# Mixture-of-experts rows gathered over two batches: 15 expert tiles per pair of batches in place of 22, with the gather and the final product one loop iteration later

## The chip, the cores and the metric

One core of a Trainium2 chip runs one program. The metric is the device time in microseconds of that core, as the median of several executions. The program is written instruction by instruction for five engines, which run in parallel and wait for each other on semaphores: TensorE (PE: matmuls and transposes), VectorE (DVE), ScalarE (ACT), GpSimd (POOL) and SyncE (SP, which here only issues DMAs). An engine takes its own instructions strictly in the order in which they are written.

## The reference

Eight batches of 512 tokens with 128 features pass two layers, everything in float32.

```python
x = L0_attn_x                                   # (8, 512, 128)
xn = _layernorm(x)
s = _L0_attn_ref(xn, Wq, bq, Wk, bk, Wv, bv)    # attention, diagonal masked
g = _silu(_L0_ffn_ref(xn, gate, W1, b1, W2, b2))  # 8 experts 128->256->128, top 2 of 8 mixed by gates
x = x + s * g
xn = _layernorm(x)
s = _L1_attn_ref(xn, ...)                       # state-space layer: rmsnorm, conv, scan over the tokens
g = _silu(_L1_ffn_ref(xn, centroids, gamma, beta, W1, b1, W2, b2))
x = x + s * g
```

The scan of `_L1_attn_ref` is, for 256 channels with 16 states each, `s = s * exp(d_t * A) + d_t * B_t * u_t` over the 512 tokens of a batch, and `y = sum over states of s * C_t`. The second experts (`_L1_ffn_ref`), which the change concerns, send each token to one of 8 experts:

```python
scores = feats @ centroids.T
expert = jnp.argmax(scores, axis=1)
alpha = jax.nn.sigmoid(jnp.sum(feats * centroids[expert], axis=-1, keepdims=True))
# per expert: layernorm, gamma, beta, 128 -> 512, relu, 512 -> 128, residual
y = the row of the token's own expert
out = alpha * y + (1.0 - alpha) * feats
```

## The kernel before

**Stages.** The work of a batch is cut into steps of five groups: A (layer norm, attention and first experts), H (projections of the state-space layer, and the choice of the second expert), S (the scan), F (the second experts) and C (the end of the state-space layer, the product and the output). The main loop has one iteration per batch: while S of batch b runs, the engines also work on A of batch b+2, H of batch b+1, F of batch b and C of batch b-1. Before the first scan stands an opening in which only A and H of the first batches run, and behind the last scan an end. I call the iteration in which batch b is scanned iteration b, 0 to 7. Iteration 6 has almost no A left and iteration 7 has neither A nor H.

**What sets the order.** A table `ROWS` gives every step a place in time and an offset for ACT, DVE and POOL, with the PSUM bank it uses. `OWN` and `OWN_BANKS` replace these for batches at the start. `PLACES` sorts all steps of all batches, and `program(engine)` is the resulting order of one engine. Nothing is decided when the program runs. There are four working banks `work0` to `work3`.

**The scan.** A batch has 32 scans, two halves h of the channels for each of 16 states n. For each, PE spreads a row of B over the partitions (`b_row`, L898), DVE multiplies (`dbu` or `b_row` by `du`, L1346), ACT makes the decays (`dA`, L988, the line of a helper that all of ACT's work has), DVE scans (L1357), and POOL multiplies by C (L1539). The rows of C are fetched from DRAM by SP (L685, tile `Cs`, three buffers). PE adds the first half in `yacc` (L915, in the last iteration L912) and POOL the second (L1546, in the last iteration PE, L938). Few state buffers exist, so a scan waits until the product of an earlier state has been added.

**The second experts.** After DVE has chosen an expert per token it computes, in step `rk` (L1307 to L1321), how many tiles of 128 rows each expert needs and at which row each token goes. 512 tokens over 8 experts need at most `ST` = (512-8)//128+8 = 11 tiles. POOL scatters the rows to `xs_dram` (L1509, four indirect DMAs, steps `put`). SP loads the tiles four at a time (L696, L670) and copies the expert's first weights within SBUF for each tile (L667, `hs<-w_w1f`). PE turns the rows (L868), multiplies (L875, eight matmul records per tile), ACT applies relu (`hsT`), PE multiplies again (L883 the bias, L885 eight records), ACT copies (`ys`), SP stores to `ys_dram` (L678), and POOL gathers the rows of the tokens back (L1526, four indirect DMAs, steps `get`, tile `fe`). ACT scales by alpha, POOL adds (L1518), ACT takes tanh, DVE finishes silu (L1334, result `g1`), and after PE's output projection (L947) DVE adds and multiplies (L1385, L1388), POOL or at the very end DVE adds the kept x (L1563, L1392), and SP stores (L709).

**Preparation.** DVE scales the weights `w1f` by gamma in SBUF (L1431), adds a bias (L1436) and splits another (L1421 to L1425). `xs_dram` is zeroed by three DMAs (L721).

## Time and profile before

| what | value |
|---|---|
| device time, median of 3 runs | 944.47 us (940.72 to 945.70) |
| the profiled execution | 945.51 us |
| its span, first to last instruction | 943.7 us |
| PE busy | 815.7 us, 86% of the span |
| DVE busy | 799.8 us, 85% |
| ACT busy | 630.5 us, 67% |
| POOL busy | 597.8 us, 63% |
| mean granted PE clock | 0.934 of 2.4 GHz |
| first scan starts, last scan ends | 123.44 us, 927.15 us |

A busy share is an average over the whole span. The windows further below give it by stage. The page counts matmuls from a model of their ends, so an engine that is shown busy for a mean of 290 ns per small matmul has issued them faster than that, and a timeline row with several in a group gives their pace. The chain that ended last goes by shares of the span: PE 42%, DVE 36%, issue 12%, ACT 5%, POOL 3%.

### The profile page before, as it was taken

How to read it: one execution, taken by the hardware profiler on the slowest of the kernel's cores; microseconds unless marked ns; L12 is line 12 of the kernel's file. 1: busy time of each engine (PE TensorE's matmuls, PEld its weight loads, DVE VectorE, ACT ScalarE, POOL GpSimd, SP SyncE). 2: the span in 40 equal slices, each digit the busy share in tenths (PEclk: the TensorE clock that was granted, in tenths of full speed). 3: DMA queues.
4: the chain of work that ended last, by engine and by line, in shares of the span. 5: the costliest groups of instructions: out<-in, count | busy, mean ns of one | idle time of the engine just before them, and what ended most of it. 6: DMA issues, size and time to landing. Idle time of an engine off the chain costs nothing.

```text
span 943.7 us, 16309 instructions
## 1 busy us (share of the span) xinstructions
PE 815.7 (86%) x4844; PEld 607.9 (64%) x4844; DVE 799.8 (85%) x1487; ACT 630.5 (67%) x1378; POOL 597.8 (63%) x564
## 2 busy tenths in 40 slices
PE   4999989986999799987899779997999876775995
PEld 3785767674686577775676657765776755563662
DVE  3345789998989979998899989899899899988995
ACT  3535678766686757776687766867677675666561
POOL 0010327578575876679584876758765797879774
PEclk9989999998999879998899979998899998977998
DMA  7300232243232431333222332324222432343441
GB/s 259 107 2 0 70 95 84 62 129 100 77 107 73 124 90 53 111 113 106 85 88 79 118 95 68 120 76 124 82 73 71 122 112 91 99 133 111 144 135 41
DMA packets 79433, 90.32 MB, mean 96 GB/s; under 512 B 8451, under 2 KB 49907, under 8 KB 78835
## 3 DMA queue, kind: packets, MB, share of 16 engines
q1 hardware_dynamic: 77298, 85.07, 29.2%
q0 software_dynamic: 2048, 4.20, 1.6%
q8 instruction: 42, 0.69, 0.3%
q14 instruction: 45, 0.36, 0.1%
HBM read 52.96 MB, written 13.04 MB: 70 GB/s over the span
## 4 chain that ended last, share of the span: by engine, by line
PE 42%; DVE 36%; issue 12%; ACT 5%; POOL 3%; DMA 1%; SPq 1%; DVEq 0%; POOLq 0%; ACTq 0%
DVE st L1357 10%; PE work L850 9%; PE work L844 9%; DVE b_row L1346 4%; PE work L777 3%; DVE cv L1270 3%; DVE acc L1241 3%; PE work L875 3%; DVE dbu L1346 2%; PE work L885 2%; PE work L761 2%; PE yacc L915 2%; PE work L768 2%; POOL st L1539 1%; PE yacc L977 1%
## 5 line engine op out<-in xcount | busy, mean ns | idle before, releaser
L1539 POOL TENSOR_TENSOR st<-st,Cs 128x512 f32<-128x512 f32 x249 | 317.2, 1280 | 161.1 <-DVE st L1357 159.3
L988 ACT ACTIVATE dA<-delta,Aneg 128x512 f32<-128x512 f32 x256 | 176.2, 722 | 14.1 <-DVE st L1357 10.4
L1357 DVE TENSOR_TENSOR_SCAN st<-dA,dbu 128x512 f32<-128x512 f32 x128 | 154.8, 1210 | 0.7 <-ACT dA L988 0.7
L844 PE MATMUL work<-xnT,w_w1a 128*128 128x512 f32 x256 | 137.2, 626 | 16.8 <-DVE delta L1327 15.0
L1357 DVE TENSOR_TENSOR_SCAN st<-dA,b_row 128x512 f32<-128x512 f32 x123 | 148.8, 1210 | 3.1 <-ACT dA L988 2.9
L850 PEld LDWEIGHTS work<-w_w2a,hid 128*128 128x128 f32 x1024 | 131.3, 205 | 18.2 <-issue 15.0
L850 PE MATMUL work<-w_w2a,hid 128*128 128x128 f32 x1024 | 134.2, 288 | 3.5 <-ACT hid L988 3.5
L1546 POOL TENSOR_TENSOR y<-y,st 128x512 f32<-128x512 f32 x105 | 133.5, 1271 | 5.2
L988 ACT ACTIVATE hid<-work,w_b1a 128x512 f32<-128x512 f32 x128 | 87.9, 688 | 66.7 <-PE work L844 60.3
L988 ACT ACTIVATE hsT<-work,hs 128x128 f32<-128x128 f32 x352 | 99.2, 372 | 45.0 <-PE work L875 45.0
L875 PEld LDWEIGHTS work<-xsT,hs 128*128 128x128 f32 x704 | 98.8, 209 | 24.3 <-DVEq L1246 9.6
L1346 DVE TENSOR_TENSOR dbu<-b_row,du 128x512 f32<-128x512 f32 x123 | 85.4, 694 | 30.8 <-PE b_row L898 22.3
L875 PE MATMUL work<-xsT,hs 128*128 128x128 f32 x704 | 104.0, 295 | 8.3 <-DVEq L1246 7.2
L885 PE MATMUL work<-w_w2f,hsT 128*128 x704 | 102.5, 290 | 0.0
L1241 DVE SCALAR_TENSOR_TENSOR acc<-work,gates,acc 128x128 f32<-128x128 f32 x256 | 71.2, 341 | 34.2 <-PE work L850 34.0
L885 PEld LDWEIGHTS work<-w_w2f,hsT 128*128 128x128 f32 x704 | 88.3, 197 | 3.2 <-issue 1.2
L1346 DVE TENSOR_TENSOR b_row<-b_row,du 128x512 f32<-128x512 f32 x123 | 83.9, 682 | 2.7
L915 PE MATMUL yacc<-w_ident,st 128*128 128x128 f32 x448 | 72.6, 291 | 3.6 <-POOL st L1539 3.6
L915 PEld LDWEIGHTS yacc<-w_ident,st 128*128 128x128 f32 x448 | 59.2, 155 | 20.4 <-issue 15.2
L1509 POOL DMA_INDIRECT xs_dram<-ht_tok,pos x32 | 32.2, 1006 | 61.8 <-DVE pos L1321 55.5
L844 PEld LDWEIGHTS work<-xnT,w_w1a 128*128 128x128 f32 x256 | 42.7, 198 | 37.1 <-DVE delta L1327 20.0
L898 PE MATMUL b_row<-bc,sel_b 96*128 96x512 bf16 x123 | 49.3, 401 | 14.3 <-DVE st L1357 14.2
(198 smaller groups left out, 1315.4 us busy)
## 6 DMA issues: line engine op xcount, KB each, us to landing
Cs<-c_dram SPq DMA_DIRECT2D x128, 256.0 KB
hs<-w_w1f SPq DMA_DIRECT2D x88, 258.0 KB, 2.3
xs_in<-xs_dram SPq DMA_DIRECT2D x16, 256.0 KB
ys_dram<-ys SPq DMA_DIRECT2D x16, 256.0 KB, 3.7
w_w1f<-in_w1f_dram SPq DMA_DIRECT2D x1, 2064.0 KB, 8.4
x_in<-in_x_dram SPq DMA_DIRECT2D x8, 256.0 KB, 3.1
w_w2f<-in_w2f_dram SPq DMA_DIRECT2D x1, 2048.0 KB, 12.2
kept_dram<-x_tok SPq DMA_DIRECT2D x8, 256.0 KB, 3.5
```

The costliest lines, as they stand in the source:

```text
L844: last = mm(w[:], W["w1a"][:, i * 128:(i + 1) * 128], xnT[:], start=True, stop=True)
L850: last = mm(w[:, t * 128:(t + 1) * 128], hid[:, c % 4, t * 128:(t + 1) * 128], W["w2a"][:, c * 128:(c + 1) * 128], start=(c == PER * i), s ...
L875: last = mm(w[:, c * 128:(c + 1) * 128], w1s[:, i % 2, c * 128:(c + 1) * 128], xsT[:, i // 4 % 2, i % 4 * 128:(i % 4 + 1) * 128], start=Tr ...
L885: last = mm(r, hsT[:, i % 2, c * 128:(c + 1) * 128], W["w2f"][:, bass.ds(e * H1 + c * 128, 128)], start=False, stop=(c == HC - 1))
L898: mm(rows_bank(n, b)[:], row_of(n), bc3[:, par], start=True, stop=True).then_inc(sig["B_in"], 1)
L915: add = mm(yacc[:, t * 128:(t + 1) * 128], state(s)[:, t * 128:(t + 1) * 128], ident[:], is_transpose=True, start=(n == 0 and t == 0), sto ...
L988: return nc.scalar.activation(out, in_, func, **k)
L1241: last = V.scalar_tensor_tensor(acc[:, t], w[:, t * 128:(t + 1) * 128], gates[:, t, i:i + 1], acc[:, t], ALU.mult, ALU.add)
L1346: V.tensor_tensor((dbu0, rows_bank(n, b))[h][:], rows_bank(n, b)[:], du[:, par, h], ALU.mult).then_inc(sig["dBu"], 1)
L1357: V.tensor_tensor_scan(state(s), dA[:, s % DECAYS], (dbu0, rows_bank(n, b))[h][:], 0.0, ALU.mult, ALU.add).then_inc(sig["scan"], 1)
L1539: G.tensor_tensor(state(s), state(s), Cs[:, b.of(NS, n) % C_BUFS], ALU.mult).then_inc(sig["P"], 1)
L1546: G.tensor_tensor(y1[:], y1[:], state(s), ALU.add).then_inc(sig["y_sum1"], 1)
```

## The change

- F now runs once per **pair** of batches. 1024 tokens need at most (1024-8)//128+8 = 15 tiles, so `ST` is 15 and there are 4 pairs in place of 8 batches: 60 tiles in place of 88.
- The rows go to a fixed place in DRAM: every expert has room for 8 tiles (`ROOM`), and the second batch of the pair continues behind the first. `xs_dram` has 71 slots, twice, and all are zeroed by 18 DMAs each, in place of 3 in all.
- After the second batch of a pair DVE computes which slot is which tile (`tile_table`: `texp`, `slot`, and the row of each token among the 15 tiles, `gpos`). `rk` of the first batch is shorter.
- SP loads each tile by a DMA of its own, with its slot read from SBUF.
- The prepared weights `w1f` are saved in DRAM (`w1f_dram`, one store of 2.1 MB) and fetched from there for each tile. Their place in SBUF then holds `g1`, two more buffers of `xn1`, two of the output `ox`, and `xr`.
- Gather, silu, product and output are a new group G, which for batch b runs in iteration b+2 (before: gather at the end of iteration b, product in b+1). G of batches 6 and 7 therefore stands at the end of the program.
- `op` only adds (into `ox`, L1483); the product is a step `fin`.
- All numbers of `ROWS`, `OWN` and `OWN_BANKS` are new. F of pair 3 and G of batches 5, 6 and 7 have tables of their own.

How many tiles' first products (L875, now L938) PE has in each iteration, counted in its order: before 11 in each of the eight; after 0, 9, 6, 9, 6, 9, 6, 15 in iterations 0 to 7.

```diff
-ST = (T - E) // 128 + E
+PAIRS = NB // 2
+ROOM = 2 * T // 128
+ST = (2 * T - E) // 128 + E
+SLOTS = E * ROOM + ST - 2 * T // 128
...
-    ("P", "dve", 0, -4.05984, 0, -9, 3, None),
+    ("P", "dve", 0, -4.69974, 0, -5, 3, None),
...
+    ("P", "save", 0, 0.01296, 1, 0, 0, None),
...
-AHEAD = {"A": 2, "H": 1, "S": 0, "F": 0, "C": -1, "P": 0}
+AHEAD = {"A": 2, "H": 1, "S": 0, "C": -1, "G": -2, "P": 0}
+COUNT = {"F": PAIRS, "P": 1}
...
+        g1, xn1_c, xn1_d, ox_a, ox_b, xr = (W["w1f"][:, k * T:(k + 1) * T].rearrange("p (i d) -> p i d", i=NT) for k in range(6))
+        ox = ox_a, ox_b
...
-                        sp.dma_start(w1s[:, k % 2], W["w1f"][:, bass.ds(e * (H1 + HC), H1 + HC)]).then_inc(w_ld[k % 2], 16)
+                        sp.dma_start(w1s[:, k % 2], w1f_dram[bass.ds(e * D, D)]).then_inc(w_ld[k % 2], 16)
...
+                        for i in group_tiles(k):
+                            r = sp.value_load(slot[0:1, par, i:i + 1], min_val=0, max_val=SLOTS - 1)
+                            sp.dma_start(xs_in[:, i % 4], xs_dram[par][bass.ds(r * 128, 128)]).then_inc(sig["xs_ld"], 16)
...
+                elif g == "P" and name == "save":
+                    sp.wait_ge(prep_dve, 3)
+                    sp.dma_start(w1f_dram.rearrange("(e d) k -> d e k", e=E), W["w1f"][:].rearrange("p (e k) -> p e k", e=E)
+                                 ).then_inc(sig["w1f_out"], 16)
+                    clear_rows(1)
+
+            def clear_rows(p):
+
+                for k in range(0, SLOTS, 4):
+                    n = min(4, SLOTS - k)
+                    sp.dma_start(xs_dram[p][k * 128:(k + n) * 128].rearrange("(i p) d -> p i d", p=128), fe[:, 0:n]
+                                 ).then_inc(sig["xs_zero%d" % p], 16)
...
+                    r = posr[:, 0:NT]
+                    lk(g, V.tensor_tensor(r, before, tiles8(W["room"]), ALU.add))
...
+                    if par:
+                        tile_table(g, b.n // 2 % 2)
...
+                elif name == "fin":
+                    dve.wait_ge(sig["g1"], b.of(1, 1))
+                    dve.wait_ge(sig["opx"], b.of(1, 1))
+                    V.scalar_tensor_tensor(ox[par], ox[par], 0.5, g1[:], ALU.mult, ALU.mult).then_inc(sig["s1"], 1)
...
+                    pair = b.n // 2
                     if i == 0:
                         for k in range(2):
-                            pool.wait_ge(ys_out[k], b.of(16 * stores_of(k), 16 * stores_of(k)))
+                            pool.wait_ge(ys_out[k], 16 * stores_of(k) * (pair + 1))
                         since(pool, sig["g1"], b.of(1))
```

**PE, at the border of iterations 1 and 2.** Between the spread of B for the last state of batch 1 (`b_row1`) and that for the first state of batch 2 (`b_row0`) stand products of the first experts (`w_w1a`, `w_w2a`), the sum of states (`yacc`), and work of the second experts. `delta` of batch 2 is made by DVE from banks `work3` and `work2` just ahead. Before:

```order
L898 MATMUL b_row1<-bc3,sel_b 128x512
L844 MATMUL work1<-xnT,w_w1a 128x512
L844 MATMUL work3<-xnT,w_w1a 128x512
L868 MATMUL work3<-w_ident,xs_in 128x128 x4
L915 MATMUL yacc<-w_ident,st 128x128 x4
L844 MATMUL work0<-xnT,w_w1a 128x512
L850 MATMUL work3<-w_w2a,hid 128x128 x8
L898 MATMUL b_row0<-bc3,sel_b 128x512
```

After:

```order
L961 MATMUL b_row1<-bc3,sel_b 128x512
L907 MATMUL work0<-xnT,w_w1a 128x512
L907 MATMUL work1<-xnT,w_w1a 128x512
L978 MATMUL yacc<-w_ident,st 128x128 x4
L938 MATMUL work0<-xsT,hs 128x128 x4
L907 MATMUL work1<-xnT,w_w1a 128x512
L913 MATMUL work0<-w_w2a,hid 128x128 x8
L978 MATMUL yacc<-w_ident,st 128x128 x4
L961 MATMUL b_row0<-bc3,sel_b 128x512
```

The first two products now go to `work0` and `work1` in place of `work1` and `work3`, and the sum of the last state has moved ahead of `b_row0`.

**DVE, at the same border.** Scans write `st`, and `acc` is the accumulation of a first expert. Before:

```order
L1346 TENSOR_TENSOR b_row1<-b_row1,du 128x512
L1357 SCALAR_TENSOR_TENSOR st<-dA,dbu0 128x512
L1357 SCALAR_TENSOR_TENSOR st<-dA,b_row1 128x512
L1346 TENSOR_TENSOR dbu0<-b_row0,du 128x512
L1346 TENSOR_TENSOR b_row0<-b_row0,du 128x512
L1357 SCALAR_TENSOR_TENSOR st<-dA,dbu0 128x512
L1241 SCALAR_TENSOR_TENSOR acc<-work3,gates,acc 128x128 x4
L1241 SCALAR_TENSOR_TENSOR acc<-work1,gates,acc 128x128 x4
```

After:

```order
L1443 TENSOR_TENSOR b_row1<-b_row1,du 128x512
L1454 SCALAR_TENSOR_TENSOR st<-dA,dbu0 128x512
L1312 SCALAR_TENSOR_TENSOR acc<-work0,gates,acc 128x128 x4
L1454 SCALAR_TENSOR_TENSOR st<-dA,b_row1 128x512
L1443 TENSOR_TENSOR dbu0<-b_row0,du 128x512
L1443 TENSOR_TENSOR b_row0<-b_row0,du 128x512
L1454 SCALAR_TENSOR_TENSOR st<-dA,dbu0 128x512
```

One accumulation has moved from behind the first scan of the iteration to ahead of the last scan of the one before.

**POOL, at the end of the program.** Indirect DMAs into `fe` are the gathers. Before:

```order
L1539 TENSOR_TENSOR st<-st,Cs 128x512 x25
L1526 DMA fe<-ys_dram,pos 128x128
L1539 TENSOR_TENSOR st<-st,Cs 128x512
L1526 DMA fe<-ys_dram,pos 128x128
L1539 TENSOR_TENSOR st<-st,Cs 128x512
L1526 DMA fe<-ys_dram,pos 128x128 x2
L1539 TENSOR_TENSOR st<-st,Cs 128x512
L1518 TENSOR_TENSOR fe<-fe,xn1_tok 128x512
```

After:

```order
L1619 DMA fe<-ys_dram,gpos 128x128 x2
L1636 TENSOR_TENSOR st<-st,Cs 128x512
L1619 DMA fe<-ys_dram,gpos 128x128
L1636 TENSOR_TENSOR st<-st,Cs 128x512
L1619 DMA fe<-ys_dram,gpos 128x128
L1610 TENSOR_TENSOR fe<-fe,w_w1f 128x512
L1619 DMA fe<-ys_dram,gpos 128x128 x4
L1624 TENSOR_TENSOR w_w1f<-w_w1f 128x512
L1610 TENSOR_TENSOR fe<-fe,w_w1f 128x512
```

The four gathers among the last products are now those of batch 6, and those of batch 7 follow them.

**DVE, at the end of the program.** `du` is the input of the last projection. After (before, one silu stood ahead of the addition that is now L1483, and one product and one sum behind it):

```order
L1474 TENSOR_TENSOR du<-yacc,zg 128x512
L1483 TENSOR_TENSOR w_w1f<-work,w_w1f 128x512
L1423 SCALAR_TENSOR_TENSOR w_w1f<-w_w1f,fe 128x512
L1427 SCALAR_TENSOR_TENSOR w_w1f<-w_w1f 128x512
L1423 SCALAR_TENSOR_TENSOR w_w1f<-w_w1f,fe 128x512
L1427 SCALAR_TENSOR_TENSOR w_w1f<-w_w1f 128x512
L1431 TENSOR_TENSOR w_w1f<-w_w1f 128x512
```

L1423 is the silu of a batch, L1427 its product, L1431 the last sum. The silu of batch 6 stands behind the projection's addition of batch 7.

**SP, at the start of iteration 0:**

```order
L748 DMA kept_dram<-x_tok 128x4x128
L738 DMA Cs<-c_dram 128x512
L762 DMA w1f_dram<-w_w1f 128x8x516
L770 DMA xs_dram<-fe 128x4x128 x17
L770 DMA xs_dram<-fe 128x3x128
L738 DMA Cs<-c_dram 128x512
```

Before, the first three fetches of C (L685) were issued in a row. Now the store of the weights and the second zeroing stand between the first and the second.

## Rows read from the trace of the kernel before

**Rows 1.** Windows: us; busy (count) of PE, PEld, DVE, ACT, POOL; clock, DMA, GB/s.

```profile
123.40:771.90 648.50, 577.14 (x3572) 437.02 (x3570) 588.54 (x1077) 469.86 (x1031) 453.84 (x422) 0.94 0.31 94
...
771.90:862.20 90.30, 61.39 (x358) 47.97 (x358) 84.82 (x128) 59.09 (x133) 73.10 (x67) 0.85 0.34 107
862.20:927.10 64.90, 58.04 (x295) 38.26 (x295) 61.15 (x71) 35.64 (x91) 49.64 (x40) 0.97 0.40 124
927.10:943.70 16.60, 8.30 (x22) 4.91 (x22) 4.95 (x8) 1.91 (x5) 6.01 (x6) 0.75 0.10 28
```

**Rows 2.** Waits of DVE, iterations 0 to 5: us in total, times, longest.

```profile
DVE dbu L1346 <- PE b_row L898: 18.6, 18, 2.3
DVE acc L1241 <- PE work L850: 8.4, 17, 1.1
DVE st L1357 <- ACT dA L988: 3.6, 8, 0.7
DVE ys L1334 <- ACT ys L988: 2.9, 2, 1.4
```

**Rows 3.** Waits of DVE, iteration 6 (771.9 to 862.2 us).

```profile
DVE dbu L1346 <- PE b_row L898: 2.4, 1, 2.4
```

**Rows 4.** Timeline, PE and DVE, border of iterations 1 and 2: start, us, idle before.

```profile
326.54 1.13 PE L844 MATMUL work<-xnT,w_w1a 128*128 128x512 f32 x2 [2.50 <-DVE delta L1327]
...
334.94 0.38 PE L898 MATMUL b_row<-bc,sel_b 96*128 96x512 bf16 x1
...
335.42 0.70 DVE L1346 TENSOR_TENSOR dbu<-b_row,du 128x512 f32<-128x512 f32 x1 [2.33 <-PE b_row L898]
```

**Rows 5.** Timeline of PE in iteration 7: the parts of one tile.

```profile
888.71 0.22 PE L883 MATMUL work<-b2p,sel_b 96*128 96x128 bf16 x1
888.77 1.11 PE L885 MATMUL work<-w_w2f,hsT 128*128 x8
...
890.79 1.05 PE L875 MATMUL work<-xsT,hs 128*128 128x128 f32 x8
```

**Rows 6.** Timeline of DVE, first and last of the 11 instructions of `rk`.

```profile
301.95 0.18 DVE L1307 TENSOR_TENSOR more<-work,w_full 128x32 f32<-128x32 f32 x1
...
304.39 0.17 DVE L1321 CAST pos<-posf 128x4 uint32<-128x4 f32 x1
```

**Rows 7.** Opening and iteration 0: DMAs saturated, preparation ends, state 1's product, eighth scan.

```profile
16.00:30.00 14.00, 13.13 (x53) 6.80 (x52) 6.62 (x24) 9.08 (x19) 0.00 (x0) 1.00 1.02 365
...
110.38 0.18 DVE L1442 TENSOR_SCALAR Aneg<-Aneg 128x32 f32<-128x32 f32 x1
...
131.59 1.28 POOL L1539 TENSOR_TENSOR st<-st,Cs 128x512 f32<-128x512 f32 x1 [3.65 <-DVE st L1357]
...
151.48 1.22 DVE L1357 TENSOR_TENSOR_SCAN st<-dA,b_row 128x512 f32<-128x512 f32 x1 [0.43 <-ACT dA L988]
```

**Rows 8.** Transfers: KB each, median us from issue to landing.

```profile
xr<-kept_dram SPq DMA_DIRECT2D x8, 256.0 KB, 3.7
...
xs_dram<-fe SPq DMA_DIRECT2D x2, 256.0 KB, 12.4
```

**Rows 9.** Timeline behind the last scan, all engines.

```profile
928.82 0.99 POOL L1526 DMA_INDIRECT fe<-ys_dram,pos  x1 [0.16 <-issue]
...
930.12 0.95 POOL L1526 DMA_INDIRECT fe<-ys_dram,pos  x1 [0.30 <-issue]
...
932.60 1.28 ACT L988 ACTIVATE fe<-fe,alpha 128x128 f32<-128x128 f32 x4 [11.16 <-DMA fe<-ys_dram,pos]
...
933.96 1.26 POOL L1518 TENSOR_TENSOR fe<-fe,xn_tok 128x512 f32<-128x512 f32 x1 [1.60 <-ACT fe L988]
...
935.25 0.63 ACT L988 ACTIVATE ys<-fe 128x512 f32<-128x512 f32 x1 [1.37 <-POOL fe L1518]
...
938.90 0.70 DVE L1385 TENSOR_TENSOR work<-work,xn_tok 128x512 f32<-128x512 f32 x1 [2.29 <-PE work L947]
...
941.07 0.39 SPq L709 DMA_DIRECT2D out_dram<-ot  x1
```

More of the change, by code:

```diff
@@ L636, in build @@
         block = ctx.enter_context(nc.Block())
-        LOADS = {"small": ["ident", "rowsel", "first", "before", "full", "tile_no", "wqT", "wkT", "wvT", "bq", "bk", "bv", "gate"],
+        LOADS = {"small": ["ident", "rowsel", "first", "before", "full", "tile_no", "room", "wqT", "wkT", "wvT", "bq", "bk", "bv", "gate"],
                  "ffn0": ["w1a", "b1a", "w2a", "b2a"],
@@ L1125, in f_step @@
                     for t in range(NT):
-                        last = go(fe[:, t], fe[:, t], ACT.Copy, scale=alpha[:, par, t:t + 1])
+                        last = go(fe[:, t], fe[:, t], ACT.Copy, scale=alpha[:, b.n % 4, t:t + 1])
                     last.then_inc(sig["r0"], 1)
```

252 lines of the change are left out of this document (143 added, 109 removed), and 571 rows, old and new, of tables (OWN, OWN_BANKS, ROWS, sig).

## The prediction

> **What bounds the kernel now.** I read the windows first, since the shares of the whole span hide the stages. From the first scan to 771.9 us, iterations 0 to 5, both PE and DVE are close to full: in 648.5 us PE is busy 577.1 us (89%) and DVE 588.5 us (91%), so DVE idles 60.0 us, ten in each iteration of about 108 us. In iteration 6, which has no A, PE is busy only 61.4 of 90.3 us (68%) and DVE 84.8 (94%). In iteration 7 it is PE that is full, 58.0 of 64.9 us [rows 1]. DVE thus carries iterations 0 to 6. The change takes no work from it, and can win there only what DVE idles because PE or ACT were late. The waits of DVE tell how much that is: 18.6 us for the spread rows of B, 8.4 for the first experts' second product, 3.6 for the decays and 2.9 for `ys`, together 33.5 us in iterations 0 to 5 [rows 2], and 2.4 us in iteration 6 [rows 3]. The other idle time of DVE is short waits on its own last results and on ACT's `cv`, which the change leaves.
>
> Of these waits one returns at each border of two iterations. PE stands 2.50 us at 326.54 before the first experts' product, because its bank `work3` still holds what DVE turns into `delta`; `b_row` of the next batch comes behind that product, at 334.94; and DVE, which has nothing in between, waits 2.33 us for it at 335.42 [rows 4]. The longest of the 18 waits for `b_row` is also 2.3 [rows 2], and the one in iteration 6 is 2.4 [rows 3]. Six borders at 2.33 and one at 2.4 are 16.4 us; what is left of the 35.9 us is 19.5.
>
> **The change, part by part.** *Fewer tiles.* A tile costs PE 1.05 us for the first product, 0.22 for the bias and 1.11 for the second [rows 5], 2.4 us together. 28 tiles fewer are 67 us of PE. But they do not leave evenly: the tiles by iteration go from 11 each to 0, 9, 6, 9, 6, 9, 6, 15. Iterations 0 to 6 lose 32 tiles, 77 us of PE, 11 us in the mean iteration; iteration 7 gains four.
>
> *The border.* The first experts' products go to `work0` and `work1`, which `delta` does not use, and one accumulation of about 1 us now stands ahead of the batch's last scan, where it gives PE time. The conflict that row 326.54 shows has no counterpart in the new order of PE, and I let all of it go: −16.4 us. Bounds: 0, if the next late thing stands in its place, and −16.4.
>
> *The rest of the waits, 19.5 us.* PE is left with (577.1 − 5.25 × 11)/648.5, about 80%, between 89% with its idle time for DVE and 68%, where beyond the border no wait for PE of any size is left [rows 1, 3]. A straight line between these two would take (89 − 80)/(89 − 68), 43%, which is 8 us. Iteration 0 has no tiles at all, and waits for a nearly full engine fall faster than its load, so I take 11 us of the 19.5; bounds 0 and 19.5. With the border that is −27 us in iterations 0 to 6.
>
> PE's clock works against this. It is 0.94 of the full one where PE is 89% busy and 0.85 where it is 68% busy [rows 1]. Along that line 80% would give 0.90, and what PE has left in an iteration of 108 us, 85 us, would take 4% or 3.6 us longer: six times that are 22 us of the 77 given back, all on PE, which still has slack. The Trainium skill, TensorE: Matmul & The Clock Gate, section on the HAM clock gate, says that the throttled clock (1.2 GHz) is the default and that activity releases it. By that rule a change that empties PE undoes some of its own gain; the trace agrees, 0.85 against 0.94 [rows 1]. What it would give as a result is the second case below.
>
> *The choice of the rows.* `rk` is 11 DVE instructions from 301.95 to 304.56, 2.6 us [rows 6], 0.24 each. Now the first batch of a pair has about 4 (0.9 us) and the second about 21 (5.0): 5.9 us per pair against 5.2. Four pairs add 2.8 us, less about 0.3 where such work fits into a wait: +2.5 us. Bounds 0 and +5.
>
> *The store and the zeroing.* They come behind the last step of the preparation, which ended at 110.56 [rows 7] and which the new table puts a little later. 2.1 MB and 18 DMAs of together 4.5 MB pass at the 365 GB/s of the saturated window [rows 7] in 18 us. Nearer in kind is a zeroing of 256 KB that took 12.4 us behind others, where a load of the same size alone took 3.7 [rows 8]. The second fetch of C stands behind all of them, so it lands between 131 and 140; before, its product ran at 131.59. The state buffer that this product frees is next wanted by the eighth scan (second half of state 3), at 151.48 [rows 7]. So up to 10 us of lateness are covered, by POOL, which idles here. I price it +1 us; bounds 0 and +10, the latter if the fetches of C that follow stay late as well. The queue's order comes first here from the program: 19 DMAs are issued ahead of it. The Trainium skill, DMA: Bandwidth & Descriptors, section Queues, rings and completion order, says that on each DMA engine the descriptors of one queue are consumed in ring order; by it the fetch of C cannot overtake the zeroing, and the 12.4 us of [rows 8] agree.
>
> The fetches of `hs` from DRAM in place of SBUF are the same bytes per tile and fewer tiles; the loads of a single tile take SP, which idles. The eight products that leave `op` become `fin`, as many DVE instructions as before. No cost.
>
> *Iteration 7.* Four more tiles on PE are 9.5 us. PE has 6.9 us idle there [rows 1]. If all of that could be filled the price were 2.6, if none 9.5. The tiles of pair 3 may be spread from the start of the iteration, but each waits for its rows and weights, so I take the middle, +5 us; bounds 2 and 9.5.
>
> *The end.* The last scan ends at 927.15, and the program 16.55 us later. The projection's addition (L1385) ended at 939.60, 12.4 us behind the scan [rows 9], and that chain stays. New is what the gathers of batch 7 wait for. POOL may write `fe` again only when batch 6's silu on DVE has read it, and that silu now stands behind the addition: 12.4 + 0.7 = 13.1. Then four gathers at 1.3 each, as 928.82 to 930.12 [rows 9]: 18.3. The last one of before landed 1.5 us after its end (931.07 to 932.60): 19.8. ACT's alpha 1.28 and a hand-over: 21.1; POOL's addition 1.26: 22.4; ACT's tanh 0.63: 23.1; three DVE instructions at 0.70 with hand-overs, 2.2: 25.3; the output's DMA, 2.6 from 941.07 to the end at 943.7: 27.9. That is 11.3 behind 16.55, +11 us. Bounds 8, if POOL's gathers are quicker with nothing beside them, and 13. The kept x of batch 7 (3.7 us [rows 8], behind its own buffer's release) lands a good 1 us ahead of need.
>
> **The sum**, on the profiled execution: 945.5 − 16.4 − 11 + 2.5 + 1 + 5 + 11 = 937.6. The median of the three runs is 1.0 below the profiled one, so I forecast 937 us (−27 + 19.5 = −7.5).
>
> **The rivals.**
>
> *The border only (948).* The slower clock and PE's own order give back what the fewer tiles free: the 11 us of the rest do not come. −16.4 + 19.5 = +3.1, so 947.6 by the median. For it: 0.85 at 68% [rows 1], and PE in iteration 7 doesn't profit at all. Against: even at 0.90 PE is 3.6 us fuller against 11 us freed.
>
> *Another wait at the border (953, slower).* The waits of DVE are from the order, not from the load. PE takes its own strictly in order, and at the border `delta`, the first products of the next A and `b_row0` all want DVE or one of four banks. The new order has `b_row0` behind eight second products into `work0` and the sum of the last state, which waits for POOL's product. If DVE again stands 2.3 us there, the 16.4 stay and only the 11 go: −11 + 19.5 = +8.5, 953. With nothing of either it would be 964. It decides from a recovery in iterations 0 to 6 below 15 us, against 19.5 us that are added elsewhere. For it: [rows 4], where all of the wait is order; iteration 6 keeps the wait of 2.4 at 68% load [rows 3]. Against: the bank conflict that caused it is gone.
>
> *The rows of C late (946).* The zeroing costs its upper end, 10 in place of 1: −7.5 + 9 = +1.5. For it: 12.4 against 3.7 [rows 8]. Against: the eighth scan's distance [rows 7].
>
> *All waits go (925).* −35.9 and an iteration 7 at its lower end of 2: −35.9 + 2.5 + 1 + 2 + 11 = −19.4. For it: iteration 6 shows almost nothing beyond the border [rows 3]. Against: it has no A to wait for.
>
> **Chances.** Forecast 0.40, border only 0.22, another wait 0.17, C late 0.08, all waits gone 0.13. Range 922 to 956: it takes in all cases' centres and leaves out the outer halves of the last and the third. The likeliest case alone has 930 to 944. A measurement of this kernel can tell some 0.5% from no change, so faster is below 939.7 and slower above 949.2. Faster: 0.32 of the forecast, all of the last case, 0.04 of the others, 0.49. Slower: most of the 0.17 and a little of the second case, 0.18. The same: 0.33.
>
> **What would show each step.** In the trace of after: no wait near 2.3 us for `b_row` where a batch's first scan starts; DVE's waits for PE in iterations 0 to 6 near 8 us in place of 36; PE's clock there about 0.90; the second fetch of C landing before 140 and no wait of the eighth scan for POOL; iteration 7 near 70 us in place of 64.9; 28 us from the last scan to the end, with the gathers of batch 7 behind batch 6's silu. I would be wrong above all if DVE has new waits, for the tiles' slots, the gathers of the older batch or the product `fin`, in the middle of the iterations, or if iteration 7 has to wait for pair 3's rows.

## The result, and the profile after

The changed kernel takes 972.08 us (median of four runs, 969.72 to 974.53), the kernel before 943.23 in the same comparison: a ratio of 1.031, with a 95% interval of 1.026 to 1.035. It is slower, by some 29 us; the prediction had 937, with 922 to 956. Its profiled execution has a span of 968.1 us, 24.4 more than before. Two of the four executions took 969.7 and 969.9 us and two 974.3 and 974.5; the profiled one is of the first two, so the table below accounts for 24.4 of the 29 us.

The windows of the changed kernel, one for the opening, one for each iteration 0 to 7 (first scan to first scan) and one from the last scan to the end (it reaches past the end of the span), columns as in [rows 1]:

```profile
0.00:127.34 127.34, 111.29 (x585) 76.08 (x586) 58.77 (x200) 65.02 (x124) 14.13 (x30) 0.96 0.36 116
127.34:240.47 113.13, 86.29 (x423) 55.19 (x423) 96.70 (x190) 62.60 (x112) 68.84 (x65) 0.80 0.37 105
240.47:340.74 100.27, 90.71 (x554) 66.38 (x554) 95.95 (x175) 73.34 (x156) 69.84 (x67) 0.97 0.32 84
340.74:449.67 108.93, 88.87 (x528) 63.28 (x527) 101.03 (x193) 71.86 (x149) 75.48 (x72) 0.92 0.27 75
449.67:554.98 105.31, 90.97 (x556) 67.30 (x555) 99.44 (x177) 74.99 (x161) 76.03 (x72) 0.95 0.32 87
554.98:669.75 114.77, 95.31 (x545) 69.78 (x546) 102.26 (x193) 71.90 (x148) 80.16 (x75) 0.88 0.27 76
669.75:774.09 104.34, 91.24 (x558) 67.10 (x557) 97.85 (x168) 76.10 (x166) 75.63 (x69) 0.95 0.32 88
774.09:866.41 92.32, 52.45 (x277) 35.63 (x275) 87.35 (x134) 50.12 (x101) 73.06 (x67) 0.72 0.31 84
866.41:938.98 72.57, 67.94 (x369) 46.55 (x369) 62.65 (x72) 41.85 (x113) 52.11 (x43) 0.97 0.50 144
938.98:1000.00 61.02, 7.42 (x20) 4.29 (x20) 6.29 (x10) 3.82 (x10) 13.01 (x12) 0.77 0.08 22
```

Beside the same stretches of the kernel before, in us:

| stretch | before | after | difference |
|---|---|---|---|
| opening | 123.4 | 127.3 | +3.9 |
| iteration 0 | 104.6 | 113.1 | +8.5 |
| iterations 1 to 6 | 634.2 | 625.9 | −8.2 |
| iteration 7 | 64.9 | 72.6 | +7.7 |
| end | 16.6 | 29.1 | +12.5 |
| span | 943.7 | 968.1 | +24.4 |

So the iterations from which I expected nearly all of the gain did get shorter, by a third of what I had, and everything around them got longer. In iterations 0 to 6 together DVE's busy time rose from 673.4 to 680.6 us, and its idle time fell only from 65.4 to 58.5.

What DVE waited for in iterations 0 to 6 of the changed kernel (us in total, times, longest):

```profile
DVE nmax L1279 <- PE work L822: 9.3, 4, 6.8
DVE st L1454 <- ACT dA L1051: 8.8, 4, 3.0
DVE acc L1312 <- PE work L913: 6.2, 6, 1.6
DVE dbu L1443 <- DVE acc L1312: 3.9, 18, 0.2
```

The waits for `b_row`, which led the list before [rows 2, 3], are gone from it but for one of 0.2 us. At the top stands one that I had not foreseen in this size, the 9.3 us of `nmax`; they all lie in iteration 0. Four waits for ACT's decays, up to 3.0 us, have come in, one near the end of each of iterations 2 to 5; before, the longest wait for a decay was 0.7 us [rows 2]. They stand 5.8 to 7.2 us ahead of the next batch's first scan, the one of iteration 2 here:

```profile
443.87 1.22 DVE L1454 TENSOR_TENSOR_SCAN st<-dA,dbu 128x512 f32<-128x512 f32 x1 [2.23 <-ACT dA L1051]
```

Iteration 0 of the changed kernel, timeline of all engines, from the store of the weights on (start, us):

```profile
123.53 0.38 SPq L762 DMA_DIRECT2D w1f_dram<-w_w1f  x1
123.60 0.18 DVE L1534 TENSOR_SCALAR Aneg<-Aneg 128x32 f32<-128x32 f32 x1
123.95 20.58 SPq L770 DMA_DIRECT2D xs_dram<-fe  x18
...
134.87 1.28 POOL L1634 TENSOR_TENSOR y<-st,Cs 128x512 f32<-128x512 f32 x1 [4.91 <-DVE st L1454]
...
144.58 0.84 SPq L738 DMA_DIRECT2D Cs<-c_dram  x1
...
149.29 2.49 POOL L1636 TENSOR_TENSOR st<-st,Cs 128x512 f32<-128x512 f32 x2 [13.14 <-DMA Cs<-c_dram]
...
150.60 1.12 PE L978 MATMUL yacc<-w_ident,st 128*128 128x128 f32 x4 [4.57 <-POOL st L1636]
...
153.57 0.69 DVE L1279 TENSOR_REDUCE nmax<-work 128x1 f32<-128x512 f32 x1 [6.80 <-PE work L822]
```

This is a chain that goes through four engines. The last step of the preparation runs at 123.60, 13 us later than before [rows 7]. The store and the 18 zeroing DMAs hold SP until 144.53, and only then is the second fetch of C issued. POOL waits for it until 149.29. PE, which takes its work in order, has the sum of that state (L978) ahead of its attention products and stops 4.57 us; and DVE, whose next instruction needs those, stops 6.80 us.

The end of the changed kernel, all engines:

```profile
951.21 0.69 DVE L1483 TENSOR_TENSOR w_w1f<-work,w_w1f 128x512 f32<-128x512 f32 x1 [3.94 <-PE work L1010]
952.04 0.69 DVE L1423 SCALAR_TENSOR_TENSOR w_w1f<-w_w1f,fe 128x512 f32<-128x512 f32 x1
...
953.60 0.95 POOL L1619 DMA_INDIRECT fe<-ys_dram,gpos  x1 [4.63 <-DVE w_w1f L1423]
...
957.36 0.94 POOL L1619 DMA_INDIRECT fe<-ys_dram,gpos  x1 [0.30 <-issue]
...
959.88 1.28 ACT L1051 ACTIVATE fe<-fe,alpha 128x128 f32<-128x128 f32 x4 [10.24 <-DMA fe<-ys_dram,gpos]
...
964.65 0.69 DVE L1431 TENSOR_TENSOR w_w1f<-w_w1f 128x512 f32<-128x512 f32 x1
```

It is the chain of the prediction, in its order: the projection's addition at 951.2, 12.2 us behind the last scan; batch 6's silu behind it; POOL's gathers of batch 7 only then; and what follows them. In [rows 9] the gathers were over at 931.07, before that addition.

### The profile page after: what moved, and what is told of

The parts are those of the page before. It is cut to its first block, busy times and chain, and to the rows that moved or that the text cites. A ratio compares the mean times of both kernels' runs of the same rounds, so it can differ in the third digit from the quotient of the medians.

```text
span 968.1 us, 15221 instructions
## 1 busy us (share of the span) xinstructions
PE 782.5 (81%) x4404; PEld 551.6 (57%) x4404; DVE 808.3 (83%) x1499; ACT 591.6 (61%) x1230; POOL 598.3 (62%) x564
## 4 chain that ended last, share of the span: by engine, by line
DVE 34%; PE 26%; issue 18%; POOL 14%; ACT 5%; SPq 2%; DMA 1%; DVEq 0%; POOLq 0%; ACTq 0%
DVE st L1454 10%; PE work L907 5%; POOL st L1636 5%; PE work L913 5%; DVE b_row L1443 3%; DVE acc L1312 3%; POOL y L1643 3%; DVE cv L1341 3%; DVE dbu L1443 2%; POOL xs_dram L1601 2%; POOL fe L1619 2%; PE work L821 2%; PE work L948 1%; PE work L1010 1%; PE work L938 1%
## 5 line engine op out<-in xcount | busy, mean ns | idle before, releaser
L907 PE MATMUL work<-xnT,w_w1a 128*128 128x512 f32 x256 | 139.5, 652 | 14.7 <-ACT hid L1051 12.4
L978 PE MATMUL yacc<-w_ident,st 128*128 128x128 f32 x448 | 78.2, 306 | 29.2 <-POOL st L1636 29.2
L978 PEld LDWEIGHTS yacc<-w_ident,st 128*128 128x128 f32 x448 | 59.5, 158 | 66.8 <-POOL st L1636 41.0
L961 PE MATMUL b_row<-bc,sel_b 96*128 96x512 bf16 x123 | 53.4, 434 | 39.9 <-DVE st L1454 39.6
L1051 ACT ACTIVATE hsT<-work,hs 128x128 f32<-128x128 f32 x240 | 67.8, 372 | 27.9 <-PE work L938 27.8
L938 PEld LDWEIGHTS work<-xsT,hs 128*128 128x128 f32 x480 | 60.1, 195 | 28.6 <-issue 12.3
L938 PE MATMUL work<-xsT,hs 128*128 128x128 f32 x480 | 65.2, 282 | 12.6 <-DMA hs<-w1f_dram 5.1
L907 PEld LDWEIGHTS work<-xnT,w_w1a 128*128 128x128 f32 x256 | 47.7, 209 | 47.6 <-issue 22.4
L948 PE MATMUL work<-w_w2f,hsT 128*128 x480 | 69.8, 290 | 0.1
L948 PEld LDWEIGHTS work<-w_w2f,hsT 128*128 128x128 f32 x480 | 60.5, 198 | 6.6 <-issue 4.9
```

The source lines that it names most:

```text
L907: last = mm(w[:], W["w1a"][:, i * 128:(i + 1) * 128], xnT[:], start=True, stop=True)
L938: last = mm(w[:, c * 128:(c + 1) * 128], w1s[:, i % 2, c * 128:(c + 1) * 128], xsT[:, i // 4 % 2, i % 4 * 128:(i % 4 + 1) * 128], start=Tr ...
L948: last = mm(r, hsT[:, i % 2, c * 128:(c + 1) * 128], W["w2f"][:, bass.ds(e * H1 + c * 128, 128)], start=False, stop=(c == HC - 1))
L961: mm(rows_bank(n, b)[:], row_of(n), bc3[:, par], start=True, stop=True).then_inc(sig["B_in"], 1)
L978: add = mm(yacc[:, t * 128:(t + 1) * 128], state(s)[:, t * 128:(t + 1) * 128], ident[:], is_transpose=True, start=(n == 0 and t == 0), sto ...
L1051: return nc.scalar.activation(out, in_, func, **k)
```

## The experiments

Twelve kernels ran. All times are medians; each is compared with runs of the kernel before on the same chip, 944.3 to 945.3 us. The changed kernel was measured only in the first comparison, where the kernel before took 943.2 us. What is said below of a run against its 972.08 us is thus a difference between two comparisons, and uncertain by 2 to 3 us: by the ratios the first run gains 12 us on it and not 9.6, the second 7 and not 4.9.

### The second zeroing spread over iteration 0

```diff
                     ).then_inc(sig["w1f_out"], 16)
-                    clear_rows(1)
...
                     sp.dma_start(Cs[:, r % C_BUFS], ...)
+                    if b.is_(0) and 3 <= k < 12:
+                        clear_rows(1, 8 * (k - 3), 8 * (k - 2))
```

> The changed kernel, with the 18 DMAs of the second zeroing no longer ahead of the second fetch of C but two at a time behind the fetches of states 3 to 11 of batch 0. Theory 1 (the queue made iteration 0 long: C of state 1 landed at 149, POOL waited 13.1 us for it, PE 4.6 us for POOL, DVE 9.3 us for PE): the second fetch lands near 133, these three waits go, iteration 0 falls from 113.1 us to about 104.6 as before, and the kernel by 8 to 9 us, to 963.5. Theory 2 (iteration 0 is long because of the new places of its steps, and POOL's wait was covered as I had forecast): the fetch lands early, but the kernel gains less than 2 us.

Measured: 962.47 us, ratio to the kernel before 1.018 (1.016 to 1.019), 9.6 us below the changed kernel. The wait of POOL for C is gone from its list, `nmax` has one wait of 0.7 us, and iteration 0 is 105.5 us long:

```profile
129.86:235.39 105.53, 82.48 (x423) 53.34 (x423) 97.95 (x190) 62.43 (x112) 68.94 (x65) 0.85 0.39 112
```

Theory 1 holds. The order on SP's queue cost 9.6 us by the medians, 7.6 of iteration 0 by the two profiles. This run also shows iterations 0 to 6 without the late rows of C: 731.6 us, 7.2 less than before, in which DVE is busy 682.6 and idle 48.9. The opening stayed long (129.9 us in this execution), so its 4 us have another source.

### A buffer of its own for the rows of batch 7

```diff
+        def fe_of(b):
+            return x_in[:, 0] if b.is_(NB - 1) else fe[:]
...
-                        since(pool, sig["g1"], b.of(1))
+                        if b.is_(NB - 1):
+                            pool.wait_ge(sig["x1"], NB)
+                        else:
+                            since(pool, sig["g1"], b.of(1))
...
     ("G", 7): (
-        8.24894, 8.32285, 8.41037, 8.59222, 9.17155,
+        8.20500, 8.20800, 8.21100, 8.21400, 9.17155,
```

> The changed kernel, with a buffer of its own for the rows of batch 7 (x_in's, free by then) and the four gathers of batch 7 ahead of batch 6's addition on POOL. Theory 1 (the gathers' wait for batch 6's silu sets the end): the gathers end near 950 in place of 958.3, the end behind the last scan falls from 29.1 us to about 22.5, the kernel by 6.5 us to 965.5. Theory 2 (POOL's last products and the output projection set it in any case): less than 2 us.

Measured: 967.20 us, ratio 1.023 (1.020 to 1.026), 4.9 us below the changed kernel. In its timeline the gathers of batch 7 (`x_in<-`) follow those of batch 6 and end at 954.59, ahead of the projection's addition:

```profile
949.90 0.94 POOL L1628 DMA_INDIRECT x_in<-ys_dram,gpos  x1 [0.30 <-issue]
...
953.65 0.94 POOL L1628 DMA_INDIRECT x_in<-ys_dram,gpos  x1 [0.30 <-issue]
...
956.03 0.69 DVE L1489 TENSOR_TENSOR w_w1f<-work,w_w1f 128x512 f32<-128x512 f32 x1 [3.94 <-PE work L1013]
...
962.99 0.69 DVE L1437 TENSOR_TENSOR w_w1f<-w_w1f 128x512 f32<-128x512 f32 x1
```

The last scan ended at 943.83 there and the span is 966.4, so the end is 22.6 us in place of 29.1, the 6.5 us expected. The median moved less since openings differ between executions (below). What is left of the end is behind batch 6's product: POOL's sum of batch 6 stands ahead of its addition for batch 7.

### Less of PE in the kernel before

```diff
-                    for c in range(HC):
+                    for c in (range(HC) if (b.is_(NB - 1) or i < 4) else (HC - 1,)):
                         last = mm(w[:, c * 128:(c + 1) * 128], w1s[...], ...)
...
-                    for c in range(HC):
+                    for c in (range(HC) if (b.is_(NB - 1) or i < 4) else (HC - 1,)):
                         last = mm(r, hsT[...], ...)
```

> The kernel before, in its own order, but of the tiles 4 to 10 of batches 0 to 6 PE does only one of four matmuls of each product (the others are left out, so their rows are not the reference's). That takes 7 x 1.6 = 11.2 us of PE from each of iterations 0 to 6, as much as the change did in the mean. Theory 1 (the step of my prediction: the waits of DVE come from PE's load): 27 us less or nearly that, about 916 us. Theory 2 (they come from the order in which PE takes its work, and PE's freed time is waited away elsewhere): less than 10 us less, 934 or more, with the wait of 2.3 us at each border still there.

Measured: 945.39 us, ratio 1.001 (0.999 to 1.002). Taking the matmuls of nearly 5 tiles out of 11 (7 tiles, 1.6 of 2.4 us each) from each of iterations 0 to 6 changes nothing that can be measured. Iteration 2, whose window of before is 109.24 us with 97.35 us of PE at a clock of 0.94:

```profile
336.83:446.06 109.23, 91.67 (x514) 65.89 (x514) 99.17 (x183) 78.40 (x174) 77.34 (x72) 0.89 0.32 94
```

PE has 84 matmul records less there, and 5.7 us less busy time, not 11.2: the clock fell from 0.94 to 0.89. The border of iterations 1 and 2, PE and DVE:

```profile
325.80 2.07 PE L844 MATMUL work<-xnT,w_w1a 128*128 128x512 f32 x2 [1.44 <-DVE delta L1327]
...
334.95 0.38 PE L898 MATMUL b_row<-bc,sel_b 96*128 96x512 bf16 x1
...
335.43 0.70 DVE L1346 TENSOR_TENSOR dbu<-b_row,du 128x512 f32<-128x512 f32 x1 [2.34 <-PE b_row L898]
```

Against [rows 4] PE arrives earlier and still waits for `delta`, 1.44 us; its two products then take 2.07 us in place of 1.13, and `b_row` comes at 334.95 as before (334.94). DVE waits 2.34 us as before (2.33). Theory 2 holds: this wait comes from the order, and what PE gained was lost to its slower clock on the same few matmuls. The Trainium skill, TensorE: Matmul & The Clock Gate, section on the HAM clock gate, has the throttled clock as the default, released by activity; these two rows agree, for products of the same shape take nearly twice as long once PE has less to do ahead of them.

### Less of PE in the changed kernel

The same edit with the condition `b.is_(PAIRS - 1)`, on all 45 tiles of pairs 0 to 2.

> The changed kernel, with one of four matmuls of each product in all tiles of pairs 0 to 2 (the others are left out). That takes another 45 x 1.6 = 72 us of PE from iterations 1 to 6, whose order stays. Theory 1 (load): iterations 1 to 6, 625.9 us now, lose 15 us or more. Theory 2 (DVE's own work, 583.9 us of the 625.9, and the order set them): 6 us or less.

Measured: 974.94 us, ratio 1.031 (1.028 to 1.033), 2.9 us above the changed kernel's median, which the two intervals don't tell apart. Iterations 1 to 6 take 630.1 us (240.33 to 870.41) in place of 625.9, and the clock of the whole is 0.857 in place of 0.893. In the runs that left these iterations as they were, they took 626 to 629 us. Less load again gives nothing; theory 2.

### The border alone, in the kernel before

```diff
-    ("A", "h", 13, 0.88651, -1, 3, -1, 3),
+    ("A", "h", 13, 0.88651, -1, 3, -1, 0),
...
-    ("A", "h", 14, 0.89746, 0, -4, -3, 0),
+    ("A", "h", 14, 0.89746, 0, -4, -3, 1),
```

> The kernel before with two numbers of its table changed: the first experts' product 13 goes to bank work0 and product 14 to work1, as in the changed kernel, in place of work3 (which delta holds) and work0. Nothing else moves. Theory 1 (the term of my prediction): PE doesn't stop 2.5 us before that product, b_row of the next batch comes 2.3 us earlier, and seven borders give up to 16.4 us, 929. Theory 2 (the border is a chain of PE, ACT and DVE in which the bank is one link of several, as in the run with fewer matmuls, where PE waited 1.44 in place of 2.50 us for the bank and DVE still 2.34): another wait takes most of its place, 4 us or less, 941.

Measured: 930.20 us, ratio 0.984 (0.981 to 0.986), 14.8 us faster than the kernel before and 42 us faster than the changed one. In iterations 0 to 6 DVE's waits for `b_row` and for the first experts' product now read

```profile
DVE dbu L1346 <- PE b_row L898: 13.4, 18, 2.8
DVE acc L1241 <- PE work L850: 6.4, 15, 1.1
```

where they had 21.0 and 8.6 us in the same stretch before [rows 2, 3]. At the border of iterations 1 and 2 the wait is gone altogether:

```profile
330.28 0.38 PE L898 MATMUL b_row<-bc,sel_b 96*128 96x512 bf16 x1
...
330.76 0.70 DVE L1346 TENSOR_TENSOR dbu<-b_row,du 128x512 f32<-128x512 f32 x1
```

Where PE no longer stops it also keeps its clock: iterations 1, 4 and 5 have a granted clock of 0.98 in place of 0.94 or 0.95, and iteration 1 is 105.34 us long in place of 108.77. The wait isn't gone at each border. At the six borders up to that of iterations 5 and 6 DVE waited 12.4 us for `b_row` before, and 3.0 are left, 1.8 of them between iterations 2 and 3. The longest wait in iteration 6 is no border's: it stands 21 us ahead of the next batch's first scan, and the two banks leave it. First before, then with the two banks:

```profile
841.49 0.70 DVE L1346 TENSOR_TENSOR dbu<-b_row,du 128x512 f32<-128x512 f32 x1 [2.38 <-PE b_row L898]
```

```profile
438.82 0.70 DVE L1346 TENSOR_TENSOR dbu<-b_row,du 128x512 f32<-128x512 f32 x1 [1.80 <-PE b_row L898]
...
829.64 0.70 DVE L1346 TENSOR_TENSOR dbu<-b_row,du 128x512 f32<-128x512 f32 x1 [2.76 <-PE b_row L898]
```

The border term of the prediction was right in mechanism and needs nothing of the rest of the change. That its 16.4 came near the 14.8 is in part luck: 9.4 us of `b_row` waits went at the borders, 2.2 of waits for the first experts' product went with them, and the rest of the gain isn't told apart.

### Gathers that needn't wait for their stores

```diff
                     pair = b.n // 2
+                    src = pair - 1 if b.n in (2, 4) else pair
...
-                            pool.wait_ge(ys_out[k], 16 * stores_of(k) * (pair + 1))
+                            pool.wait_ge(ys_out[k], 16 * stores_of(k) * (src + 1))
...
-                    G.indirect_dma_start(fe[:, i], None, ys_dram[pair % 2]...
+                    G.indirect_dma_start(fe[:, i], None, ys_dram[src % 2]...
```

> The changed kernel, in which the gathers of batches 2 and 4 read the rows of the pair before (complete long since) and wait for that pair's stores, so those two batches get other rows than the reference's. Order and work stay. In the changed kernel POOL waits 6.2 us in iteration 4 for the last store of pair 1. Theory 1 (this wait is what makes iteration 4, 114.8 us, longer than iteration 2 of the same table, 108.9): iteration 4 falls by 5 us, the kernel by 5 to 6, 966.5. Theory 2 (POOL makes it up, DVE's own 102 us and the order set the iteration): less than 2 us.

Measured: 972.85 us, ratio 1.030 (1.027 to 1.032), no gain. Iteration 4 is 113.6 us. POOL's waits in it, in the changed kernel

```profile
POOL fe L1619 <- DMA ys_dram<-ys: 6.2, 1, 6.2
```

and here

```profile
POOL st L1637 <- DMA Cs<-c_dram: 6.1, 1, 6.1
```

The same 6 us, at the same place, now for the rows of C. SP's own timeline of that run:

```profile
631.82 0.37 SPq L731 DMA_DIRECT2D ys_dram<-ys  x1
632.24 1.89 SPq L738 DMA_DIRECT2D Cs<-c_dram  x1
```

The fetch of C stands on SP behind the very store for which POOL waited before, and SP waits for the tiles of that store. Taking away POOL's wait uncovers SP's. What iteration 4 would gain if both went was not tried.

### Iteration 7: PE, the tiles' loads, and both

Three kernels, all from the changed one. First, matmuls left out in the last six tiles (condition `i < 9 or not b.is_(PAIRS - 1)`):

> The changed kernel; of the last six tiles of the last pair (9 to 14) PE does one of four matmuls of each product. That takes 6 x 1.6 = 9.6 us of PE from iteration 7, as much as the four tiles that it has more than before. Theory 1 (iteration 7 is bound by PE, 67 of 72.6 us busy): iteration 7 falls by 6 us or more, 966. Theory 2 (PE's clock and the order give it back, as in the two runs with fewer matmuls): 2 us or less.

Measured: 970.99 us, ratio 1.027 (1.025 to 1.029). Iteration 7:

```profile
871.18:943.94 72.76, 63.06 (x297) 39.50 (x297) 63.37 (x72) 41.65 (x113) 52.03 (x43) 0.93 0.51 144
```

Nothing gained. Second, one DMA for a group of tiles:

```diff
-                        for i in group_tiles(k):
-                            r = sp.value_load(slot[0:1, par, i:i + 1], min_val=0, max_val=SLOTS - 1)
-                            sp.dma_start(xs_in[:, i % 4], xs_dram[par][bass.ds(r * 128, 128)]).then_inc(sig["xs_ld"], 16)
+                        n = len(group_tiles(k))
+                        sp.dma_start(xs_in[:, 0:n], xs_dram[par][k * 512:k * 512 + n * 128].rearrange("(i p) d -> p i d", p=128)
+                                     ).then_inc(sig["xs_ld"], 16 * n)
```

> The changed kernel, with one DMA for each four tiles from a fixed place of xs_dram in place of one DMA per tile with its slot read from SBUF (so the tiles hold other rows than the reference's). It frees about 3 us of SP per group. Theory 1 (in iteration 7 the weights of a tile come late because SP is behind: PE waits 1.05 and 0.75 us for hs before the b_row that DVE waits 3.51 us for): iteration 7 falls from 72.6 to 68 or less, the kernel by 5 us. Theory 2 (the weights are late because their buffer comes free late, or iteration 7 is long by its order): less than 2 us.

Measured: 972.57 us, ratio 1.030 (1.027 to 1.032). Iteration 7 fell to 70.4 us in the profiled execution, the kernel did not. Third, both, with all 15 tiles of the last pair light:

> The changed kernel with one DMA per four tiles from a fixed place (as in the run before this one) and one of four matmuls of each product in all 15 tiles of the last pair (the others are left out): 24 us less of PE and some 11 us less of SP in iteration 7. With six light tiles alone iteration 7 stayed at 72.8 us, with the loads alone it fell to 70.4. Theory 1 (PE and the feeding of its tiles hide each other; together they are the +7.7 us): 65 us or less, as before the change. Theory 2 (iteration 7 is set by DVE's 62.3 us, ACT and the new order): 68 or more.

Measured: 962.42 us, ratio 1.021 (1.017 to 1.024), 9.7 us below the changed kernel. Iteration 7:

```profile
868.67:933.03 64.36, 52.62 (x189) 26.27 (x189) 61.77 (x72) 42.19 (x113) 52.49 (x43) 0.96 0.56 162
```

It is as short as before the change, and DVE waits only 0.2 us for PE in it. In the changed kernel the largest such wait looks like this, PE and DVE:

```profile
897.20 1.13 PE L938 MATMUL work<-xsT,hs 128*128 128x128 f32 x8 [1.05 <-DMA hs<-w1f_dram]
899.08 1.13 PE L938 MATMUL work<-xsT,hs 128*128 128x128 f32 x8 [0.75 <-DMA hs<-w1f_dram]
900.04 0.38 PE L961 MATMUL b_row<-bc,sel_b 96*128 96x512 bf16 x1
...
900.46 0.70 DVE L1443 TENSOR_TENSOR dbu<-b_row,du 128x512 f32<-128x512 f32 x1 [3.51 <-PE b_row L961]
```

Two tiles' weights are late, `b_row` stands behind them, and DVE waits 3.51 us. With the group's single load the wait in that place was 1.48 us. So the 15 tiles of iteration 7 cost 7 to 8 us through two things together, their matmuls and their feeding; the run of both edits doesn't divide them, since it also lightened the nine tiles that the first run left as they were. PE is busy 52.6 us there, less than the 58.0 of before, so it doesn't show either that 15 full tiles with better feeding would fit into 64.9 us.

### Three mends together

The spread zeroing, batch 7's own buffer, and

```diff
             sp.wait_ge(prep_dve, 1)
+            sp.wait_ge(loads["ffn1"], 16 * len(LOADS["ffn1"]))
             clear_rows(0)
```

> The changed kernel with three mends together: the second zeroing spread over iteration 0, the first zeroing only once all weights have landed, and the buffer of its own for the rows of batch 7 with its gathers earlier. If the costs stand side by side they add: 9.5 and 5 us by the two runs so far, and for the first zeroing 3 us if it is what makes the opening 4 us longer (0 if that is the new order's): 955 to 958. If one cost hides another, 962.

Measured: 958.55 us, ratio 1.016 (1.011 to 1.020), 13.5 us below the changed kernel. The first two costs add (9.6 + 4.9 = 14.5). The opening was still 127.85 us, so nothing shows that the first zeroing is what lengthens it. Of the changed kernel's variants that leave nothing out this is the best, and still slower than before.

### Less and more of PE, once more

With the border edit in the kernel before, the light tiles again:

> Both edits in the kernel before: the two banks at the border, and one of four matmuls of each product in tiles 4 to 10 of batches 0 to 6 (the others are left out). It tells whether PE's load counts once the border no longer hides it. Theory 1 (with the bank conflict gone the 11 us less of PE per iteration come through, as my prediction had it): 10 us or more below the border edit alone, 920 or less. Theory 2 (DVE's own work, its order and PE's lower clock leave nothing for it): 930, within 3 us of the border edit alone.

Measured: 929.39 us, ratio 0.984 (0.981 to 0.986), 0.8 us below the border edit alone. In the profiled execution iterations 1 to 6 are 4.9 us shorter (618.8 against 623.7), and opening, iteration 7 and end 2.8 us longer. That is the most that any run here shows for some 78 us of matmuls.

And in the kernel before, more of PE:

```diff
-                    for c in range(HC):
+                    for c in list(range(HC)) * (1 if b.is_(NB - 1) or i < 4 else 2):
                         last = mm(w[:, c * 128:(c + 1) * 128], w1s[...], ...)
```

> The kernel before; the four matmuls of the first product of tiles 4 to 10 of batches 0 to 6 are done twice, the second time over the first, so PE has 7 x 1.05 = 7.4 us more in each of iterations 0 to 6. Theory 1 (PE's load sets DVE's waits): 15 us slower or more, 960. Theory 2 (PE still has that much to give): 5 us or less. If taking 11 us away gives nothing and adding 7 costs much, the load sits just below a threshold and the prediction's straight line was the wrong shape; if both do nothing, only the order counts.

Measured: 950.54 us, ratio 1.006 (1.004 to 1.008), 5.5 us slower for 52 us of matmuls more. Iterations 1 to 4 hardly moved (109.3 to 109.6 us, before 108.8 to 109.5), with the clock up at 0.97; iteration 5 took 109.0 us in place of 107.1, and iteration 6, which bears most of it, 95.1 in place of 90.3. So PE's load sets little in iterations 1 to 5 in either direction: the clock takes up part of what is added or removed, and PE's waits for other engines the rest.

## Why the prediction was wrong

By its own steps, each in us:

- **The border, −16.4.** Right in mechanism, with a reading that was wrong: the six borders held 12.4 us, and the 2.4 in iteration 6 that I added is no border's wait. In the kernel before, the two bank numbers give 14.8. In the changed kernel the `b_row` waits of [rows 2, 3] are gone, but at four of the borders a scan now waits for ACT's decays, 8.8 us in all where such waits came to 3.6.
- **The rest of the waits, −11.** Wrong, and the costliest step. It was read off a straight line between PE's busy share in two stages and DVE's waits. But iteration 6 differs from the others by having no A, not only by its load: A is what PE, ACT and DVE hand to each other. The runs with fewer matmuls in iterations 0 to 6 give 0 (interval from −0.7 to +1.7 us on the ratio), +2.9 and −0.8. Waits between engines that each take their own work in a fixed order didn't go with the load of one of them. I had put the clock's share at 22 of 77 us "all on PE, which still has slack"; [rows 4] against the light run shows that it falls on the matmuls ahead of `b_row`, where there is none. (The sum had a slip too: iterations 0 to 5 lose 27 tiles, 65 us of PE, not 58. PE was busy 84% there, not 80.) What border and rest came to together is seen in the run with the zeroing spread, since the late rows of C are out of it. There the waits of [rows 2, 3] that I counted on, 36 us, are down to 14: 22 less, where I had 27. But DVE's idle time fell only from 65.4 to 48.9 us, 16.5 less: smaller waits took the place of a part of them.
- **The choice of the rows, +2.5.** Mis-sized, and not by a count of instructions. DVE is 7.2 us busier in iterations 0 to 6, and 9.2 in the run with the zeroing spread. Some of its instructions take up to 1.8 us longer than their like, and each of these ends right behind an instruction of POOL. POOL and DVE of the changed kernel, in order of their starts:

```profile
302.46 1.27 POOL L1636 TENSOR_TENSOR st<-st,Cs 128x512 f32<-128x512 f32 x1 [0.50 <-DVE st L1454]
302.66 1.12 DVE L1258 TENSOR_TENSOR eq<-eq,w_first 128x32 f32<-128x32 f32 x1
303.69 1.26 POOL L1643 TENSOR_TENSOR y<-y,st 128x512 f32<-128x512 f32 x1
304.03 0.96 DVE L1260 TENSOR_TENSOR ohr<-eq,gr 128x32 f32<-128x32 f32 x1
```

  `eq` (L1258) ends at 303.78, 0.05 us behind POOL's product, and `ohr` at 304.99, 0.04 behind POOL's sum. In iteration 0, while POOL stood waiting for C, the same L1258 took 0.19:

```profile
142.50 0.19 DVE L1258 TENSOR_TENSOR eq<-eq,w_first 128x32 f32<-128x32 f32 x1
```

  I counted every instruction of DVE that took over 0.4 us more than the shortest of its line, tiles and shape. Before there are 31, together 27 us too long; after there are 42, 38 us. Each ends 0.03 to 0.10 us behind a product or sum of POOL that ran beside it, the ones of 128x512 some 0.55 us behind it. In iterations 0 to 6 they make 25.6 us before and 36.3 after, which is more than all by which DVE got busier. So a part of DVE's "busy" is DVE held up beside POOL, and the new order has more of these meetings: `alpha` (L1373) is hit in six of eight batches, before in one. Most of DVE's instructions ran beside POOL's at their usual length; why these are hit the traces don't say, and no run moved them apart.
- **The store and the zeroing, +1.** Wrong by its cover: 9.6 by the first run (7.6 in its profile), close to the upper bound of 10. Two things failed. I let the preparation end "a little later" than 110.56; it ended at 123.6, and the whole queue moved with it, so that C landed at 149 and not at 131 to 140. And I named only the scan that needs the state's buffer, at 151.48 [rows 7], as the one who waits. The first to wait was PE, in whose order the sum of that state stands ahead of the attention products. The Trainium skill, DMA: Bandwidth & Descriptors, section Queues, rings and completion order, has descriptors of a queue consumed in ring order on each DMA engine, which is not an order of completion, so "cannot overtake" said too much. What held C here came a step earlier: SP had not issued the fetch before 144.58, being busy 20.6 us with 18 DMAs, 1.14 us each.
- **Iteration 7, +5.** Right in direction, measured +7.7. The bounds of 2 and 9.5 held it. The feeding of the tiles was missing from its reasons.
- **The end, +11.** Right in mechanism, measured +12.5 in the profiled execution. The gathers began 14.6 us behind the last scan in place of 13.1: the addition ended 0.5 us later than I had it, and POOL began 0.9 us after the silu's end.
- **The opening, 0.** Missed: +3.9 in the profiled execution. Over the profiled executions of the changed kernel and its variants the first scan starts between 127.1 and 130.9 us, in those of the kernel before and its variants between 123.3 and 125.1. Holding the first zeroing back didn't shorten it; the new order of the opening wasn't tried apart, and the cause stays open.

My rival for slower (953) named another wait at the border, for `b_row` once more. That one didn't come, but another did: ACT's decays, 1.8 to 3.0 us, at four of the borders. And its mark, a recovery in iterations 0 to 6 below 15 us, was met: 7.2 us without the late C. The kernel is slower because these iterations gave some 7 to 9 us in place of 25, DVE having 9 us more to do or to sit out beside POOL and its idle time falling by 16.5 in place of 27, and because the costs around this, of which I had seen all but one, came to 33.7 in place of 17 (opening 3.9, C 9.6, iteration 7 7.7, end 12.5). The rival "the rows of C late" was the true one for its term, with a chance of 0.08, but it was priced alone; together with "the border only" it gives 948 + 9 = 957, already outside the range. Cases that don't exclude each other should have been combined.

## What to carry to other kernels

Where engines take their own instructions in a fixed order and hand work to each other, taking load from the second busiest engine can give nothing, as here, where the waits of the busiest one come from the order: follow the longest repeated wait back to its cause first. Here that was one PSUM bank, two numbers in a table, 14.8 us. Don't take busy time for work: compare the lengths of like instructions, and look at what runs beside the long ones. When a change puts a batch of transfers into an issuing engine's order, take as its start the new place of what releases it, count each issue at its own time, and look for the first instruction on any engine that stands behind the delayed one, not for the last one that needs it. And a stage that is moved behind the end of a pipeline pays its whole chain there, once for each buffer that it shares with the batch ahead.

## What the runs showed of the hardware

- The granted clock of TensorE followed its load in both directions and damped it: in iteration 2 of the kernel before 0.89 with 514 matmul records, 0.94 with 598 and 0.97 with 654, and PE busy 91.7, 97.4 and 99.4 us. It also followed stalls: with the bank conflict gone, the same 598 records ran at 0.98 in iteration 1, where they had 0.95, and took 93.2 us in place of 96.3.
- 18 zeroing DMAs in a row behind a store of 2.1 MB held SP 20.58 us, 1.14 us for each (17 of 256 KB and one of 192). Two at a time between the fetches of C, in the first run, they took 0.97 to 1.04 us a pair. So the 1.14 is not the price of issuing one by itself.
- 31 instructions of DVE before and 42 after took over 0.4 us longer than their like, ones of 15 elements too, and every one ended 0.03 to 0.10 us (of 128x512: some 0.55 us) behind a sum or product of POOL that ran beside it. With POOL idle the same instruction took 0.19 us in place of 1.12.
